# Weights of the feed-forward part turned by DMA transposes instead of by TensorE, and residual rows moved from SyncE's to GpSimd's DMA queue

## What is computed

```python
x = _layernorm(x + _L0_attn_ref(x, ...), axis=-1)                       # Hyena block
x = _layernorm(x + _L0_xattn_ref(ctx_2048, ctx_2048, x, ssm_kernel, D, 8), axis=-1)
x = _layernorm(x + _L0_ffn_ref(x, w1, w2), axis=-1)

def _bitlinear(x, w):
    rms = rsqrt(maximum(mean(w * w), EPS))
    w_quant = clip(round(w * rms), -1.0, 1.0) / rms
    scale = 127.0 / maximum(max(abs(x), axis=-1, keepdims=True), EPS)
    x_quant = clip(round(x * scale), -128.0, 127.0) / scale
    return einsum('bsd,fd->bsf', x_quant, w_quant)
```

## Time and profile before

| | before |
|---|---|
| median of 3 runs | 1066.54 us (1066.52 to 1067.28) |
| profiled execution | 1063.69 us, span 1061.9 us |
| TensorE busy, share of span | 1006.2 us, 95% |
| VectorE | 799.3 us, 75% |
| ScalarE | 599.9 us, 56% |
| GpSimd | 552.7 us, 52% |
| output stage of the second half | from 389.2 us to 459.9 us |

### The profile page before, as it was taken

How to read it: one execution, slowest core, us unless ns; L and a number is a source line. 1 busy time by engine, 2 the same in 40 slices (tenths; PEclk the granted TensorE clock), 3 DMA queues, 4 the chain that set the end, 5 groups by cost and what they waited for, 6 DMA issues and landing times.

```text
span 1061.9 us, 14827 instructions
## 1 busy us (share of the span) xinstructions
PE 1006.2 (95%) x4679; PEld 602.9 (57%) x4679; DVE 799.3 (75%) x1509; ACT 599.9 (56%) x728; POOL 552.7 (52%) x886
## 2 busy tenths in 40 slices
PE   3899999999999999978999999999999999999985
PEld 2455545544445555456666666666666666666641
DVE  7967975786475567657888888888888888888862
ACT  5655544112566558114666666767576767676664
POOL 5320310221000004269787887878787878787861
PEclk9999999999999999989999999999999999999998
DMA  9323655456475777441444544444444444444334
GB/s 322 61 60 120 203 152 163 145 165 194 162 227 189 241 259 255 141 143 51 105 98 113 105 113 108 115 106 117 104 117 105 109 114 101 122 99 114 76 64 91
DMA packets 178220, 144.65 MB, mean 136 GB/s; under 512 B 99988, under 2 KB 132792, under 8 KB 176120
## 3 DMA queue, kind: packets, MB, share of 16 engines
q1 hardware_dynamic: 178168, 144.00, 49.3%
HBM read 89.29 MB, written 33.70 MB: 116 GB/s over the span
## 4 chain that ended last, share of the span: by engine, by line
PE 50%; DVE 2%; POOL 1%; ACT 1%; DMA 1%; issue 1%; POOLq 0%; DVEq 0%; ACTq 0%
PE conv_bank L1398 28%; PE hq_bank L1421 9%; PE ff_bank L1442 5%; PE back_bank L1442 5%; PE back_bank L1412 1%; PE back_bank L1381 1%; PE ctx_bank L1369 1%; DMA hq_t<-hq_int 0%; POOL sum L1742 0%; DVE z L1607 0%; DVE g_max L1674 0%; POOL sum L1744 0%; ACT g L1546 0%; DMA xq_t<-xq_int 0%; ACT hq_f L1507 0%
## 5 line engine op out<-in xcount | busy, mean ns | idle before, releaser
L1742 POOL TENSOR_TENSOR sum<-z 128x640 f32<-128x640 f32 x128 | 198.2, 1549 | 11.6 <-DVE z L1619 9.6
L837 DVE SCALAR_TENSOR_TENSOR conv_all<-u,taps,conv_all 128x1024 f32<-128x1024 f32 x92 | 122.4, 1331 | 93.2 <-ACT conv_all L708 91.4
L1398 PE MATMUL conv_bank<-block_diag 128*128 128x288 f32 x628 | 167.8, 411 | 1.8 <-DVE z L1619 1.8
L1398 PE MATMUL conv_bank<-kv,block_diag 128*128 128x288 f32 x640 | 168.6, 406 | 0.9 <-DVE z L1619 0.8
L1398 PEld LDWEIGHTS conv_bank<-kv,block_diag 128*128 128x128 f32 x640 | 117.8, 190 | 31.6 <-DVE z L1619 1.8
L1398 PEld LDWEIGHTS conv_bank<-block_diag 128*128 128x128 f32 x628 | 117.3, 193 | 32.4 <-DVE z L1619 2.2
L1421 PE MATMUL hq_bank<-x_lo,hq_t 128*128 128x512 f16 x512 | 122.2, 382 | 4.7 <-DMA hq_t<-hq_int 4.7
L1674 DVE TENSOR_REDUCE g_max<-g 128x1 f32<-128x512 f32 x128 | 85.8, 673 | 41.5 <-ACT g L1546 41.5
L700 ACT ACTIVATE u<-slot_bank,bias,unscale 128x1024 f32<-128x1024 f32 x46 | 55.4, 1204 | 108.9 <-PE slot_bank L509 88.6
L1744 POOL TENSOR_TENSOR sum<-sum 128x320 f32<-128x320 f32 x128 | 111.3, 869 | 10.0
L1607 DVE TENSOR_TENSOR z<-conv_bank,qx 128x512 f32<-128x512 f32 x128 | 88.0, 687 | 34.2 <-PE conv_bank L1398 24.6
(11 more groups left out here) (181 smaller groups left out, 1676.2 us busy)
## 6 DMA issues: line engine op xcount, KB each, us to landing
x_quad<-in_w SPq DMA_DIRECT2D x10, 1024.0 KB, 8.3
v_scratch<-conv_all SPq DMA_DIRECT2D x16, 512.0 KB, 3.5
c_scratch<-v_tok SPq DMA_DIRECT2D x8, 1024.0 KB, 5.3
y<-c_scratch SPq DMA_DIRECT2D x8, 1024.0 KB, 4.9
res<-in_x SPq DMA_DIRECT2D x32, 256.0 KB, 2.9
x_scratch<-res SPq DMA_DIRECT2D x32, 256.0 KB, 3.1
block_diag<-in_ctx SPq DMA_DIRECT2D x32, 256.0 KB, 3.7
block_diag<-ssm_scratch SPq DMA_DIRECT2D x32, 256.0 KB, 3.7
```

Source lines behind the costliest of these rows:

```text
L837: ins = nc.vector.scalar_tensor_tensor(out=acc, in0=(u_first[kind] if n < 3 else u)[:, t0 + tap:t0 + tap + T // 2, :].rearrange("p t b -> ...
L1398: last = nc.tensor.matmul(view(conv_bank[tb % 2][:, hh, :], 0, (ROW64, T // 2), (1, PAIRS)), toep[:, head.buf, (tb - sb_) * P:(tb - sb_ + ...
L1742: nc.gpsimd.tensor_tensor(sum2[:, :, :], z[:, b, :, 0:half], z[:, b, :, half:2 * half], ALU.add).then_inc(sum2_done, 1)
```

## The change

The rounded and clipped part is no longer turned by TensorE. ScalarE packs its lower halves into a dense fp16 tile in SBUF (`pack_part`, one operation of 128x2048 for a part, into the room of the part before it or of `v_tok`), and SyncE turns the tile with one DMA transpose into `w1_t` or `w2_t` (`turn_part`, part i behind row 2 + i of SyncE's loop). `w1_t` is laid out with the 512 columns of one (k, dc) next to each other. SyncE waits for all eight transposes at the end of its block. The context of the first two heads is reversed between the parts (`REVERSE_AT`) and `CTX_AT` goes from 11 to 9.

In the second half the loads of rows 19 to 31 and the stores of rows 16 to 31 are issued by GpSimd: after the factor of row R comes the store of row R - 1 and then the load of row R + 3. The store of row 31 comes last. They have semaphores of their own (`late_loaded`, `late_stored`).

```diff
@@ SyncE
+                def turn_part(i):
+                    if i == 0:
+                        sp.wait_ge(slot_full, HALF * NSLOT)
+                    sp.wait_ge(packed, i + 1)
+                    if i < PARTS:
+                        out = view(w["w1_t"], i * DC * 512, (P, FC), (1, P))
+                    else:
+                        out = view(w["w2_t"], (i - PARTS) * P, (D, FC), (1, P))
+                    sp.dma_start_transpose(out, part_int[i]).then_inc(part_done, 16)
...
                     for t in range(T):
                         R = hf * T + t
-                        if R + 3 < HALF * T:
+                        if hf + 1 < HALF:
                             load_res(R + 3)
-                        store_res(R)
+                            store_res(R)
...
+                        if hf + 1 == HALF and t in TURN_PART_AT:
+                            turn_part(TURN_PART_AT[t])
+                sp.wait_ge(part_done, 2 * PARTS * 16)
@@ TensorE
-                def turn_part(i):
-                    pe.wait_ge(clipped, i + 1)
...
-                            last = nc.tensor.transpose(out[:, j * P:(j + 1) * P], low[:, fc * P:(fc + 1) * P], w["ident16"][:, :])
-                        last.then_inc(part_turned, 1)
...
-                        if hf + 1 == HALF and t in PART_AT:
-                            turn_part(PART_AT[t])
@@ ScalarE
-                def copy_part(i):
...
+                def pack_part(i):
+                    act.wait_ge(clipped, i + 1)
+                    if i == 0:
+                        act.wait_ge(c_stored, 16 * HALF * DC)
+                    else:
+                        act.wait_ge(packed, i)
+                    low = view(part_raw[i].bitcast(F16), 0, (2, F))
+                    if i < PARTS:
+                        out, src = view(part_int[i], 0, (DC * P, DC), (P, DC), (1, P)), view(low, 0, (2 * P, DC), (2 * D, DC), (2, P))
+                    else:
+                        out, src = part_int[i], low
+                    nc.scalar.activation(out, src, ACT.Copy, bias=-HALF_ONE).then_inc(packed, 1)
@@ VectorE, res_stat
-                    dve.wait_ge(res_loaded[i], 16 * (R // 4 + 1))
+                    if R < T + 3:
+                        dve.wait_ge(res_loaded[i], 16 * (R // 4 + 1))
+                    else:
+                        dve.wait_ge(late_loaded[i], 16 * ((R - T - 3) // 4 + 1))
@@ GpSimd
+                def load_res(R):
+                    hf, t = divmod(R, T)
+                    if R < T + 4:
+                        pool.wait_ge(res_stored[R % 4], 16 * (R // 4))
+                    else:
+                        pool.wait_ge(late_stored[R % 4], 16 * (R // 4 - T // 4))
+                    nc.gpsimd.dma_start(res[:, R % 4, :], dram["x"][t, b_rows(hf), :]).then_inc(late_loaded[R % 4], 16)
+
+                def store_res(R):
+                    hf, t = divmod(R, T)
+                    pool.wait_ge(res_normed, R + 1)
+                    nc.gpsimd.dma_start(dram["x1_scratch"][t, b_rows(hf), :], res[:, R % 4, :]).then_inc(late_stored[R % 4], 16)
...
-                        res_rstd_of(hf * T + t)
+                        R = hf * T + t
+                        res_rstd_of(R)
+                        if not more:
+                            if t >= 1:
+                                store_res(R - 1)
+                            if R + 3 < HALF * T:
+                                load_res(R + 3)
+                store_res(HALF * T - 1)
```

More of the change, by code:

```diff
@@ L128, in hyena_block @@
                     view(u[:, :, :], 0, (1, F)), view(conv_all[:, :, :, :], X0 * F, (1, F))]
+        part_int = [view(home, 0, (1, F // 2)).bitcast(F16) for home in (v_tok[:, :], *part_raw[:-1])]
         turn_bank = [view(early["conv_bank"][i // 2][:, i % 2, :], 0, (P, 4), (1, P)) for i in range(4)]
@@ L159, in hyena_block @@
         out_full = sem("out_full")
+        late_stored = early["late_stored"]
+        late_loaded = [sem(f"late_loaded{i}") for i in range(4)]
         res_loaded = [sem(f"res_loaded{i}") for i in range(4)]
@@ L204, in hyena_block @@
         rounded = sem("rounded")
-        part_turned = sem("part_turned")
+        packed = sem("packed")
         part_done = sem("part_done")
@@ L217, in hyena_block @@
         CLIP_AT = {i - 1: i for i in range(2, 2 * PARTS)}
-        PART_AT = {1 + i: i for i in range(2 * PARTS)}
-        CTX_AT, PAIRS_AT = 11, 12
+        TURN_PART_AT = {2 + i: i for i in range(2 * PARTS)}
+        CTX_AT, PAIRS_AT = 9, 12
+        REVERSE_AT = {3: 0, 6: 1}
         TURN_AT = {4: 1, 9: 2, 14: 3}
@@ L587, in sum_matrix @@
                     nc.tensor.matmul(turn_bank[0][:, 0, 0:2], ones[:, :], total[:, :], start=True, stop=True).then_inc(summed, 1)
-                def turn_part(i):
-                    pe.wait_ge(clipped, i + 1)
[L591 to L599, removed]
-                            last = nc.tensor.transpose(out[:, j * P:(j + 1) * P], low[:, fc * P:(fc + 1) * P], w["ident16"][:, :])
-                        last.then_inc(part_turned, 1)
                 def turn_first_ctx():
                     pe.wait_ge(early["ctx_reversed"], 1)
-                    pe.wait_ge(part_done, 2 * (2 * PARTS - 2) + 1)
+                    pe.wait_ge(ch_copied, 4 * HALF * DC)
                     for lb in range(LB):
@@ L614, in convolve_first @@
                         pe.wait_ge(early["kv_done"], 1)
-                        pe.wait_ge(part_done, 2 * 2 * PARTS)
                     for sb_ in range(tb + 1):
@@ L794, in _ @@
                         round_part(i + 2)
[L795 to L798, removed]
+                    pack_part(i)
+                    if i in REVERSE_AT:
+                        h = REVERSE_AT[i]
+                        act.wait_ge(early["ctx_loaded"][h], 16)
+                        reverse_blocks(nc, early, h).then_inc(early["ctx_reversed"], 1)
                 act.wait_ge(early["ctx_turned"], 1)
@@ L1323, in _ @@
                 for i in range(4):
-                    sp.wait_ge(early["res_stored"][i], 16 * (HALF * T // 4))
+                    sp.wait_ge(early["late_stored"][i], 16 * (T // 4))
                 def turn_xq(head):
@@ L1441, in ffn1 @@
                     for dc in range(DC):
-                        last = nc.tensor.matmul(bank[:, :], xq_t[:, dc, :], w["w1_t"][:, dc, k * 512:(k + 1) * 512],
+                        last = nc.tensor.matmul(bank[:, :], xq_t[:, dc, :], w["w1_t"][:, k, dc, :],
                                                 start=(dc == 0), stop=(dc == DC - 1))
@@ L1808, in build @@
         }
-        w["w1_t"] = w["x_hi"][:, :, :]
+        w["w1_t"] = view(w["x_hi"][:, :, :], 0, (DC * 512, F // 512), (512, DC), (1, 512))
         w["w2_t"] = w["x_lo"][:, :, :].rearrange("p c (k e) -> p (c k) e", e=D)
@@ L1826, in build @@
         early["res"] = sb("res", [P, 4, D])
+        early["late_stored"] = [ctx.enter_context(nc.semaphore(f"late_stored{i}")) for i in range(4)]
         early["res_stored"] = [ctx.enter_context(nc.semaphore(f"res_stored{i}")) for i in range(4)]
```

## The result

The changed kernel takes 1089.24 us (median of 4 runs, 1086.90 to 1093.10) against 1066.53 us: a ratio of 1.0226, 95% interval 1.0201 to 1.0252, so 22.7 us slower. The forecast was 1091.7 us. The profiled execution took 1086.90 us, its span is 23.1 us longer, and this stretch alone accounts for it: from the first row matmul to the first transposition of the next block it was 70.7 us before (389.18 to 459.93 us; the end is in rows 2) and is 95.0 us now. It starts 1.3 us earlier than before, and what follows it lasts as long as before (602.2 us against 602.0).

The account below looks back on a forecast made before the run. The output rows were held to have no slack on the load side, each load waiting for a store. 403.2 + 12 x 5.7 + 2 + 3 + 8.5 = 485.1 against 459.9: +25.2, so 1091.7 us; 8 in 10: 1073 to 1110.

Parts of the forecast that it names:

- TensorE's 7.2 us: Second half's output rows: turning 8 parts at 0.9 us leaves TensorE; counted as 0, since TensorE was not held to pace rows.
- A serial step on GpSimd that replaces the row: Output rows: factor, store issue, wait for landing and load issue follow in order on GpSimd, 5.7 us against 3.5.
- a step under 4.1 us: Sign that the prediction is wrong: a row's step on GpSimd in the output stage below 4.1 us.
- The size of that step, 5.7 us: GpSimd's row: factor 1.08, store issue 0.9, landing 2.7, load issue 0.9, hand-over 0.1 us; range 4.5 to 7.0.
- The estimate of 2.6 us for issue and landing together: Alternative for a 256 KB store from GpSimd: 2.6 us for 0.9 + 2.7, making the total 12 us smaller.
- The crowded DMA engines, 2 us: Output stage: 1 MB parts up to about 415 us, plus the transposes, delay landings; 2 us in all (1 to 4.5).
- The clips, 3 us: Six VectorE clips beside GpSimd's factor or store issue hold GpSimd up: 0 to 6.6 us, half taken, 3 us.
- The end of the stage, 8.5 us: Row 31's load to next block: 7.0 us before, plus 0.6 for load issue and 0.9 for the last store.
- TensorE's clock: Rival: clock falls in TensorE's pauses between rows, +15 us, 1107 us or more; over 1108, with dearer issue or lock, 0.13.
- The cheap round trip: Rival: GpSimd's step is below TensorE's 3.5 us, so the 7.2 us count: 1059.3 us; faster, chance 0.05.
- the break-even of 4.1: GpSimd's row step of about 4.1 us, near which the change measures as nothing; within 0.2%, chance 0.03.

## Why the prediction was right, and which of its numbers were not

*TensorE's 7.2 us count nothing.* Right. They came through only in the run with eight buffers, and there the transposes took them back.

*A serial step on GpSimd that replaces the row.* Right, and the decisive step: the run with the queue alone has it, and the run that waits for an older store takes about half of the loss away. The prediction had named a step under 4.1 us as a sign of being wrong; the quiet step of 4.2 us cleared that only just.

*The size of that step, 5.7 us.* Too large: 4.2 us quiet. The issue of the load is 0.55 us, not 0.9, the factor some 0.9 and not 1.08, and the store, whose issue takes 0.74 us, lands 2.5 us after the start of that issue (the profile's median for GpSimd's queue; the next load starts 0.3 us later), not after 0.9 + 2.7 = 3.6. Twelve steps of 4.2 instead of 5.7 are 17.8 us less than I summed. The estimate of 2.6 us for issue and landing together, by the Trainium skill's page "DMA: Bandwidth & Descriptors", section "Anatomy of one DMA — SWDGE (gpsimd) path", would have been the better term: the trace has 2.5.

*The crowded DMA engines, 2 us.* Far too small: this is the term that was most mis-sized. From the first load to the last, 401.77 to 472.25, it was 70.5 us; less twelve quiet steps of 4.22 this leaves 19.8 us. 7.9 us are in the first step (12.1 us, the store behind the 1 MB parts; 10.8 and 11.1 in the runs without transposes), 4.4 us in the second, and 1.8 to 2.0 us in each of the next four; all but the first vanish with the transposes. The transposes were priced too low themselves, with landing at some 4.6 us (3.1 + 1.5) where the median was 6.3 us and the first took 17.4. Their issue, 1.7 to 15.3 us, cost nothing only because SyncE had nothing else to do.

*The clips, 3 us.* Nothing, by the run without transposes. The rule of the Trainium skill, page "SBUF — State Buffer", section "SBUF: two separate sides", which I set against it, would have GpSimd locked out during the clips. The factor's first step agrees: it took 1.38 us instead of 0.24 in the one row in which it met a clip. For the issue of a DMA it was hardly tested: the store's issue took the same 0.73 to 0.74 us with and without a clip, but each clip began only in the last 0.2 us of it (436.69 against 436.15 to 436.89), and in no run did GpSimd begin to issue a DMA inside a clip. So in this kernel the clips cost no step; the rule itself is neither shown nor refuted.

*The end of the stage, 8.5 us.* It was 10.6; the pause at the end of GpSimd's block was not in my sum.

The four errors nearly cancel: 1.4 us from the earlier start, 17.8 from the step, against 14.8 from the crowd and clips (19.8 for 5) and 2.1 from the end; 2.25 us are left (485.1 against 482.85). The forecast missed by 2.5 us, and it owes that to chance; its range, which held the bounds of each term, is what the working supports.

*The rivals.* TensorE's clock did fall: 0.50 granted (1.2 GHz) from 422 to 428 us, behind a pause of 6.6 us, and the two rows there took 5.0 us each on average. VectorE waited 20.9 us for loads and 0.6 us for TensorE, so it cost nothing here. The cheap round trip did not come: 4.2 us lies above the 3.5 us of TensorE and just above the break-even of 4.1. By that step alone the loss would have been some 5 us; about half of the 24.2 us came from the crowd, through the same wait, and 3.6 us from the end.

## What to carry to other kernels

Before a DMA is moved to another engine's queue, ask what that engine does next: a wait that costs little on an engine with nothing else to do becomes a step of the row on one that makes a factor. If a load waits for the store issued just ahead of it, more buffers or a load placed elsewhere is the remedy, and here memory that was no longer read gave four. Work taken from a full engine is a gain only if the one that receives it, here DMA engines and a queue, is not full in the same stretch.

## What the runs showed of the hardware

- A DMA transpose of 128x2048 fp16 kept SyncE's queue for 2.7 to 4.2 us in the run with the transposes alone, where the DMA engines' share was 0.96 from 415 to 450 us, and for 15.3 us in the changed kernel, where the first was issued behind several MB; the same instruction for 128x1024 took 1.25 us in the next block. In the changed kernel it landed after 5.5 us at the least and 6.3 in the median (17.4 the first).
- A DMA of 256 KB issued by GpSimd takes it 0.55 us (load, 0.81 the first) or 0.54 to 0.74 us (store), and lands in a median of 3.0 and 2.5 us, against 2.9 and 3.1 for SyncE's in the kernel before.
- Where GpSimd issued the last store of its block, its first instruction of the next block came 3.4 us after that issue, in five profiles; where it issued none at the end, 1.3 to 1.4 us after its last factor (2.4 in the run with the last four stores on SyncE's queue).
